# Early-fusion block on one core: inputs handed over in the engines' layout, embedding as six full tiles

## What is computed

```python
patches = im.reshape(B, C, gh, ph, gw, pw).transpose(0, 2, 4, 1, 3, 5).reshape(B, gh * gw, C * ph * pw)
embeds = jnp.einsum('bsp,pd->bsd', patches, W) + b + pos          # 768 values a patch, 192 out
h = jnp.concatenate([cls_tok, embeds, txt], axis=1)
Q = xn[:, None] * W_qk[None, :, None, :]
attn = softmax(causal(Q @ Q.T / sqrt(E)))
out = (attn @ (xn - mean(wte, axis=0))) * N_reg                   # wte: 50257 x 192
h = h + out @ W_o.T
h = h + ffn(layernorm(h))
```

## Time and profile before

| | us |
|---|---|
| median of 3 runs | 526.26 |
| lowest, highest | 524.65, 526.41 |
| profiled execution | 524.14 |
| its span | 522.3 |

### The profile page before, as it was taken

How to read it: one execution, slowest core, us unless ns; L and a number is a source line. 1 busy time by engine, 2 the same in 40 slices (tenths; PEclk the granted TensorE clock), 3 DMA queues, 4 the chain that set the end, 5 groups by cost and what they waited for, 6 DMA issues and landing times.

```text
span 522.3 us, 8913 instructions
## 1 busy us (share of the span) xinstructions
PE 480.4 (92%) x2776; PEld 409.0 (78%) x2776; DVE 332.0 (64%) x868; ACT 178.8 (34%) x575; POOL 66.3 (13%) x93
## 2 busy tenths in 40 slices
PE   0689999999999999999799998779999999999995
PEld 0556666896669866697566997779999999999994
DVE  5584477716675376634863856976666666666764
ACT  0044745604556244733233013312322232223221
POOL 4011111031102011100000143000000000000000
PEclk9977899999999999999987996989999999999997
DMA  9999999489993999995000000011111111111103
GB/s 167 280 177 174 216 214 215 88 158 213 213 211 56 207 213 211 213 203 107 0 1 0 2 20 1 0 31 28 35 38 38 28 35 40 35 28 35 29 1 85
DMA packets 38618, 52.84 MB, mean 101 GB/s; under 512 B 14929, under 2 KB 31318, under 8 KB 38340
## 3 DMA queue, kind: packets, MB, share of 16 engines
q0 software_dynamic: 7664, 39.98, 37.2%
q1 hardware_dynamic: 27612, 10.64, 9.8%
q10 hardware_dynamic: 3320, 1.95, 2.0%
HBM read 50.08 MB, written 1.09 MB: 98 GB/s over the span
## 4 chain that ended last, share of the span: by engine, by line
PE 82%; DVE 10%; ACT 2%; issue 2%; ACTq 1%; DMA 1%; POOL 1%; DVEq 0%
PE bank L930 13%; PE bank L825 11%; PE bank L783 6%; PE bank L729 5%; PE bank L899 4%; PE bank L901 4%; PE bank L902 4%; PE bank L900 4%; PE bank L903 4%; PE bank L731 4%; PE bank L788 3%; PE bank L741 2%; PE bank L742 2%; PE bank L757 2%; PE bank L702 2%; PE bank L691 2%
## 5 line engine op out<-in xcount | busy, mean ns | idle before, releaser
L930 PE MATMUL bank<-wdn,hidT 128*128 128x192 f32 (+1 forms) x408 | 78.9, 330 | 5.9 <-DVE hidT L1179 5.9
L615 ACT ACTIVATE area_b<-bank,bcol 128x356 f32<-128x356 f32 x68 | 38.0, 558 | 132.3 <-PE bank L903 132.3
L1359 DVE SCALAR_TENSOR_TENSOR R<-bank,wts,R 128x192 f32<-128x192 f32 (+1 forms) x204 | 72.6, 411 | 8.2 <-issue 3.6
L930 PEld LDWEIGHTS bank<-wdn,hidT 128*128 128x128 f32 (+1 forms) x408 | 67.6, 184 | 6.5 <-DVE hidT L1179 6.5
L529 ACT ACTIVATE pm<-bank,nmax 128x128 f32<-128x128 f32 x96 | 33.9, 365 | 113.0 <-DVE nmax L1088 113.0
L825 PE MATMUL bank<-woT,oT 128*128 128x192 f32 (+1 forms) x432 | 71.6, 327 | 0.0
L1179 DVE SCALAR_TENSOR_TENSOR hidT<-bank,bcol,area_b 128x356 f32<-128x356 f32 x68 | 40.0, 588 | 48.8 <-PE bank L903 48.8
L825 PEld LDWEIGHTS bank<-woT,oT 128*128 128x128 f32 (+1 forms) x432 | 69.9, 182 | 0.5
L899 PE MATMUL bank<-xah,wah 128*128 128x356 f32 x136 | 54.3, 399 | 0.4 <-DVE lg L1137 0.4
L443 POOL DMA_DIRECT2D wacc<-in_L_attn_wte_dram x26 | 31.5, 1263 | 117.5 <-DMA wacc<-in_L_attn_wte_dram 117.5
L901 PE MATMUL bank<-xah,wal 128*128 128x356 f32 x136 | 45.2, 332 | 0.0
(11 more groups left out here) (197 smaller groups left out, 801.7 us busy)
## 6 DMA issues: line engine op xcount, KB each, us to landing
wacc<-in_L_attn_wte_dram POOLq DMA_DIRECT2D x28, 1344.0 KB, 12.9
wdn<-in_L_ffn_Wd_dram SPq DMA_DIRECT2D x16, 96.0 KB, 1.9
wacc<-wacc POOLq DMA_DIRECT2D x1, 1344.0 KB, 9.6
wra<-in_L_ffn_Wu_dram SPq DMA_DIRECT2D x16, 64.0 KB, 1.8
wrb<-in_L_ffn_Wu_dram SPq DMA_DIRECT2D x32, 32.0 KB, 2.0
wra<-in_L_ffn_Wg_dram SPq DMA_DIRECT2D x16, 64.0 KB, 2.0
wrb<-in_L_ffn_Wg_dram SPq DMA_DIRECT2D x32, 32.0 KB, 2.0
R<-in_L_attn_W_o_dram SPq DMA_DIRECT2D x2, 384.0 KB, 14.0
```

What stands on the lines that cost most here:

```text
L930: last = pe.matmul(o, hidT[:, sl, at:at + rows], wdn[:, k, :], start=True, stop=True)
L1359: last = dve.scalar_tensor_tensor(out=old, in0=src, scalar=wts[0:rows_, 3 * i + t, bass.ds(e, 1)], in1=old, op0=ALU.mult, op1=ALU.add)
```

## The change

The host hands over six inputs in another order of axes. The patches come as `x[pair]`: 128 partitions by six blocks of 128 columns (the 768 values of a patch cut into six, 49 patches of one image and 49 of the other at column 64); the patch weights, the positions (as a table with one row for each output row), the head scales, the text and `W_o` come as they lie in SBUF. So `shift_in`, the turns at L678 to L682, `output_weights` and ScalarE's copies are gone, and each is loaded by one DMA or a few. `embed` is six matmuls of 128 rows, 128 columns of patches and 192 outputs for each pair of images. TensorE starts with 16 matmuls of the mask into a PSUM bank that the first scores overwrite. The query area's memset is on GpSimd instead of VectorE; VectorE clears R's four tail tiles, which `W_o` used to fill. The table's first load waits for `woT` and stands behind the first `rstd`; ten, nine and seven additions replace eight, eight and ten. The reduction into `wbar` is five additions, one behind each of the first five groups of the last pair.

TensorE, start of the program, before: `wqk` and `posx` are the head scales and positions, `z` the normalised rows.

The core of the diff:

```diff
@@ -289,42 +277,26 @@
...
-        def image_in(queue, b):
-
-            for c in range(C):
-                at = (0, PS, 4 * PS)[c]
-                queue.dma_start(ximg[at:at + PS, b].rearrange("p (g w) -> p g w", g=G),
-                                x[b, c].rearrange("(g p) w -> p g w", p=PS)).then_inc(s_x[b // 2], 16)
-            queue.dma_start(ximg[5 * PS:6 * PS, b].rearrange("p (g w) -> p g w", g=G)[:, :, 0:WI - HALF],
-                            x[b, C - 1].rearrange("(g p) w -> p g w", p=PS)[:, :, HALF:WI]).then_inc(s_x[b // 2], 16)
-
...
             def text_in(n, b0, b1):
-                sp.dma_start(hin[NIMG:P, b0:b1, 0, :], txt[b0:b1, 0:TM, :].rearrange("b t e -> t b e")).then_inc(s_text[n], 16)
-                sp.dma_start(hin[0:TAIL, b0:b1, 1, :], txt[b0:b1, TM:NTXT, :].rearrange("b t e -> t b e")).then_inc(s_text[n], 16)
-
-            image_in(sp, 0)
+                sp.dma_start(hin[NIMG:P, b0:b1, 0, :], txt[0:TM, b0:b1, :]).then_inc(s_text[n], 16)
+                sp.dma_start(hin[0:TAIL, b0:b1, 1, :], txt[TM:NTXT, b0:b1, :]).then_inc(s_text[n], 16)
+
+            sp.dma_start(ximg[:, 0], x[0]).then_inc(s_x[0], 16)
             sp.wait_ge(s_zero, 1)
             text_in(0, 0, 2)
             sp.dma_start(hin[NIMG - 1:NIMG, :, 0, :], tok_cls[0].rearrange("a (c e) -> a c e", c=1)
                          .broadcast_to([1, B, E])).then_inc(s_text[0], 16)
-            for b in range(2, B, 2):
-                image_in(sp, b)
+            sp.dma_start(ximg[:, 1], x[1]).then_inc(s_x[1], 16)
             text_in(1, 2, B)
-            tails = txt[:, TM:NTXT, :].rearrange("(i k) t e -> k t i e", k=2)
+            for i in range(2, PAIRS):
+                sp.dma_start(ximg[:, i], x[i]).then_inc(s_x[i], 16)
             for k in range(2):
-                sp.dma_start(htail[TAIL * k:TAIL * k + TAIL, :, :], tails[k]).then_inc(s_text[1], 16)
-
-            for part, rows in ((0, P), (1, 64)):
-                src = W_o[P * part:P * part + rows, :].rearrange("o (q j e) -> o q j e", q=NH // 2, j=2)
-                dst = wo_raw[part][0:rows].rearrange("o (q c) e -> o q c e", c=3)
-                for j in range(2):
-                    sp.dma_start(dst[:, :, j, :], src[:, :, j, 0:P]).then_inc(s_wo, 16)
-                    sp.dma_start(dst[:, :, 2, 64 * j:64 * j + 64], src[:, :, j, P:E]).then_inc(s_wo, 16)
+                sp.dma_start(htail[TAIL * k:TAIL * k + TAIL, :, :], txt[TM:NTXT, k::2, :]).then_inc(s_text[1], 16)
+            sp.dma_start(woT[:], W_o).then_inc(s_wo, 16)
...
@@ -434,6 +406,14 @@
             own.mark(pool.tensor_tensor(nregf[:], nregf[:], shift[:], ALU.add))
             pool.wait_ge(pool_own, own.at)
             pool.memset(wts[:], 1.0).then_inc(s_const, 1)
+            pool.wait_ge(s_const, 1)
+            pool.memset(qb[64:P], 0.0).then_inc(s_pad, 1)
+            pool.wait_ge(s_pad, 3)
+
+            def rstd(n, count):
+
+                pool.wait_ge(var_ready, count)
+                pool.tensor_tensor(rs[:, 0:n], ve[:, 0:n], mhalf[:, 0:n], ALU.pow).then_inc(rstd_ready, 1)
 
             def add_rows(c):
...
@@ -445,26 +425,20 @@
                 else:
                     pool.dma_start(wacc[:, side], wte_v[c]).then_inc(wte_in[side], 16)
 
-            pool.wait_ge(s_x[0], 128)
-            pool.wait_ge(s_tokw, 64)
+            rstd(4, 1)
+            pool.wait_ge(s_wo, 16)
             pool.dma_start(wrest[0:WREST, :], wte[P * WROWS:V, :]).then_inc(wte_rest, 16)
-
-            def rstd(n, count):
-
-                pool.wait_ge(var_ready, count)
-                pool.tensor_tensor(rs[:, 0:n], ve[:, 0:n], mhalf[:, 0:n], ALU.pow).then_inc(rstd_ready, 1)
 
             add_rows(0)
             add_rows(1)
-            rstd(4, 1)
             rstd(4, 2)
-            for c in range(2, 10):
+            for c in range(2, 12):
                 add_rows(c)
             rstd(4, 3)
-            for c in range(10, 18):
+            for c in range(12, 21):
                 add_rows(c)
             rstd(4, 4)
-            for c in range(18, NCHUNK):
+            for c in range(21, NCHUNK):
                 add_rows(c)
             for side in range(2):
...
 
         @block.scalar
         def _(act):
-            for g in range(2):
-                src = tok_W.rearrange("(q g k) e -> g q k e", g=2, k=HALF)[g]
-                act.dma_start(wtok[2 * PS * g:2 * PS * g + 2 * PS], src[0:2 * PS]).then_inc(s_tokw, 16)
-                act.dma_start(wtok[4 * PS + PS * g:5 * PS + PS * g], src[2 * PS:PATCH]).then_inc(s_tokw, 16)
-            image_in(act, 1)
-            act.dma_start(posr[:, 0, :], tok_pos[0, 0:P].rearrange("d h w -> d (h w)")).then_inc(s_pos, 16)
-            act.dma_start(posr[0:64, 1, :], tok_pos[0, P:E].rearrange("d h w -> d (h w)")).then_inc(s_pos, 16)
-            act.dma_start(tokb[:, 0:1], tok_b[0:P].rearrange("(e a) -> e a", a=1)).then_inc(s_pos, 16)
-            act.dma_start(tokb[0:64, 1:2], tok_b[P:E].rearrange("(e a) -> e a", a=1)).then_inc(s_pos, 16)
-            act.dma_start(wqk[:], W_qk).then_inc(s_small, 16)
+            act.dma_start(wtok[:], tok_W).then_inc(s_tokw, 16)
+            act.dma_start(w2[:], W_qk.rearrange("p (c h) -> p c h", c=2)).then_inc(s_small, 16)
+            act.dma_start(postab[:], tok_pos).then_inc(s_pos, 16)
+            act.dma_start(tokb[:], tok_b.rearrange("(a e) -> a e", a=1).broadcast_to([P, E])).then_inc(s_pos, 16)
             act.dma_start(lnw[:], ln_w.rearrange("(a e) -> a e", a=1).broadcast_to([P, E])).then_inc(s_small, 16)
-            for b in range(3, B, 2):
-                image_in(act, b)
 
             def turn_out(b, bt):
...
@@ -559,16 +525,12 @@
...
-            act.wait_ge(s_w2, 2)
+            act.wait_ge(s_w2, 1)
...
             queries_b(0, 0, [2])
-            for c in range(0, NCH, 2):
-                act.wait_ge(s_wops, c // 2 + 1)
-                act.activation(woT[:, c:c + 2, :], bank[4 + (c // 2) % 2][:, 0:2 * E].rearrange("p (c e) -> p c e", c=2),
-                               ACT.Copy).then_inc(s_woT if c + 2 < NCH else proj_read, 1)
             act.wait_ge(xnT_ready, 4)
...
@@ -674,37 +636,18 @@
...
-            pe.wait_ge(s_small, 32)
-            pe.transpose(bank[7][:, 0:NH], wqk[:, 0:P], ident[0:NH, 0:NH])
-            pe.transpose(bank[7][0:64, NH:2 * NH], wqk[:, P:E], ident[0:NH, 0:NH]).then_inc(s_wqps, 1)
-            pe.wait_ge(s_posx, 1)
-            pe.transpose(bank[4][:, 0:P], posx[:, 0, :], ident[:])
-            pe.transpose(bank[4][:, P:E], posx[0:64, 1, :], ident[0:64, 0:64]).then_inc(s_posps, 1)
+            for _ in range(WARM):
+                pe.matmul(bank[0][:, :], identb[:], cmask[:].rearrange("p (a t) -> p a t", a=1).broadcast_to([P, GRP, P]),
+                          start=True, stop=True)
 
             def embed(i):
 
-                pe.wait_ge(s_x[i], 128)
-                pe.wait_ge(s_shift, i + 1)
-                for k in range(HALF):
-                    for half in range(2):
-                        tokens = ximg[:, 2 * i + half, k:k + PS * (G * G - 1) + 1:PS]
-                        last = pe.matmul(emb_bank[i][64 * half:64 * half + G * G, 0:E], tokens, wtok[:, k, :],
-                                         start=(k == 0), stop=(k == HALF - 1))
+                pe.wait_ge(s_x[i], 16)
+                for k in range(KX):
+                    last = pe.matmul(emb_bank[i][:, 0:E], ximg[:, i, k, :], wtok[:, k, :], start=(k == 0), stop=(k == KX - 1))
                 last.then_inc(s_embps, 1)
 
-            def output_weights():
-                pe.wait_ge(s_wo, 16 * 8)
-                pe.wait_ge(s_hin, 2)
-                for c in range(NCH):
-                    if c >= 4 and c % 2 == 0:
-                        pe.wait_ge(s_woT, c // 2 - 1)
-                    for part, rows in ((0, P), (1, 64)):
-                        last = pe.transpose(bank[4 + (c // 2) % 2][:, (c % 2) * E + part * P:(c % 2) * E + part * P + rows],
-                                            wo_raw[part][0:rows, c, :], ident[0:rows, 0:rows])
-                    if c % 2:
-                        last.then_inc(s_wops, 1)
-
-            pe.wait_ge(s_tokw, 64)
+            pe.wait_ge(s_tokw, 16)
             embed(0)
             embed(1)
...
@@ -835,7 +779,6 @@
             scores(0, 0)
             embed(2)
             embed(3)
-            output_weights()
 
...
@@ -886,7 +829,7 @@
...
-            pe.wait_ge(s_woT, NCH // 2 - 1)
+            pe.wait_ge(s_wo, 16)
             pe.wait_ge(s_hin, PAIRS)
...
@@ -996,51 +939,30 @@
...
             dve.memset(hin[:, :, 1, :], 0.0).then_inc(s_zero, 1)
-            own.mark(dve.memset(posx[:], 0.0))
             own.mark(dve.memset(lg[:], 0.0))
             own.mark(dve.memset(scan[:], 0.0))
             own.mark(dve.memset(mv[:], 1.0))
             dve.memset(xb[64:P], 0.0).then_inc(s_pad, 1)
             dve.memset(pT1[:], 0.0).then_inc(s_pad, 1)
-            dve.memset(qb[64:P], 0.0).then_inc(s_pad, 1)
-            dve.wait_ge(dve_own, own.at)
```

(61 more changed lines are left out.)

69 lines of the change are left out of this document (32 added, 37 removed).

## The result

| | before | after |
|---|---|---|
| median, us | 526.34 (4 runs, 524.65 to 527.54) | 502.09 (4 runs, 501.91 to 502.19) |
| profiled execution, us | 524.14 | 502.05 |
| its span, us | 522.3 | 500.2 |

The ratio of after to before is 0.9541, with a 95% interval of 0.9515 to 0.9568: 4.6% faster. The forecast was 503.7 us, its sum 502.6 for the profiled execution.

What follows compares the result with a forecast made beforehand. TensorE, busy 92% of the span, was taken as the bound, so only its waits, slow spells and removable work pay. 8.1+1.4+8.5-1.5+5.0 = 21.5 us off 524.14 gave 502.6, put at 503.7 us, range 498 to 510.

Steps and rivals of the forecast that it cites:

- Start: Program start to VectorE's first embedding addition: at 13.9 instead of 22.0 us, 8.1 us gained, bounds 5.2 and 8.9.
- The memset's move: Query area's memset from VectorE to GpSimd at the start: 4 to 6 us there, done by 12, effect zero.
- Embeddings of images 4 to 7: Behind the first scores: 24 passes take 3.9 instead of 5.38 us, 1.4 us gained on VectorE's chain.
- output weights: Ahead of the second scores: transposes and copies go, and VectorE's 8.51 us wait with them; 8.5 us gained.
- A new slow spell: Behind the second scores TensorE has little work and its clock falls: -1.5 us, bounds 0 and -3.
- Last pair: Five hidden additions replace the output weights' reduction: 5.0 us gained (3.5 waiting, 1.5 clock), at least 2.
- rival 4: Last pair's additions not hidden: 0.76 us of each comes back, 3.8 at most, 507.5 us; chance 0.05.
- GpSimd and the table: Reordered GpSimd queue: third root at 96, its user at 111, covered by 15 us; no effect on time.
- Rival 1: TensorE's clock stays up, neither slow spell occurs: 499.7 us, 498 with the early start bound; chance 0.2.
- the first spell: TensorE's slow clock at the first scores, 5.2 us at half pace; rival 1 took 2.5 us for its absence.
- Rival 2: The 16 matmuls fail to raise the clock, or data land late: 506.6 to 509.6 us; chance 0.2.
- Profiled against median: Sum of 502.6 us raised to 503.7, since before's median stood 2.1 above its profiled execution.

Runs made afterwards that it cites:

- three base kernels: After without the 16 matmuls, constants awaited later, memset first, token counts later: 499.39 us; plus twelve matmuls behind the second embedding, 497.57; or third embedding moved there, 495.85.
- an experiment alone: Kernel before with only the output weights loaded in their final layout by one DMA, without transposes and copies: 517.3 us, ratio 0.9809.
- the second trace: The unchanged kernel after, profiled and timed once more: 501.22 us, ratio 0.9542, span 499.9.
- The experiment: Kernel after with 15 instead of 10 table additions ahead of GpSimd's third reciprocal root: 518.41 us, ratio 0.9876.

## Why the prediction was right, and where it was not

*Start (8.1 predicted, 8.56 measured).* The size was right: the matmuls took 5.45 us where 6.0 were taken, the embedding 1.96 where 2.0 were taken. The view behind it was only half read. The prediction took the 16 matmuls as the given start and looked whether data were in time for them (by 9). It never asked what the start would be without them: the first pair's data are in at 5.5 to 6.1 us (landing by about 9 had been worked out; the second pair's are in at 10.6 to 11.2), and the matmuls delay an embedding that could already run. They cost 5.45 us, and the higher pace gives back 1.67 at the first embedding and 0.3 at the second (12 passes in 2.22 us without the matmuls, in 1.94 with them). In the three base kernels the two embeddings took 2.5, 3.3 and 4.4 us longer than in after, which is more than those 2.0 and still less than 5.45. The term could have been 2.8 us larger in a kernel that doesn't have them; for the kernel as it is, the estimate stands. The memset's move was put at zero and came out at zero, but by the matmuls' cover: on GpSimd it held a VectorE operation up for 3.6 us, which the prediction did not foresee; VectorE was ready at 10.61, 2.83 us before the embedding was.

*Embeddings of images 4 to 7 (1.4; 1.30)* and *output weights (8.5; 8.49)* hold, the second one shown by an experiment alone (7.86). The output weights landed by 26.03 us, inside the 21 to 33.5 worked out from the page's rates (20.4 and 33.2 when the sum is redone), and TensorE's only wait ahead of the loop was 1.33 us for VectorE.

*A new slow spell (-1.5; -1.69).* Right as a price, but not a property of the kernel: it was there in after's first trace and absent in its second one. The sum charged it in full, with 0 as a bound, for the gap behind the second scores; the same gap stood in the second trace without the spell, so the gap alone does not bring it. That the profiled execution paid it is luck, and so is part of how well the sum fits it: in an execution that is spared the spell, this term is off by 1.5 us.

*Last pair (5.0; 5.15)* holds in both directions, and all additions were hidden: rival 4 did not occur.

*GpSimd and the table (0; 0).* The third root was issued at 93.68 where 96 was worked out, its user came at 111.03 where 111 was. (The addition ahead of the root, which the prediction calls the eleventh, is the tenth, seven steps behind the third as its sum has it, and 46+7x6.9 is 94.3; it stood at 92.92.) The experiment shows that the cover is 15.8 us and what happens beyond it.

*Rival 1* did not come about in after, but its price for the first spell was borne out when the gap ahead of it was filled (2.47 of 2.5 us). *Rival 2* had its two causes wrong for this kernel: data and output weights were early, and the 16 matmuls sufficed in every trace. That little was in reserve is right: at 6.42 us they were close to the 6.9 that all 16 take at the low clock, and the embedding behind them still took 1.96 us.

*Profiled against median.* The prediction added 1.1 us to the sum because before's median stood 2.1 above its profiled execution. In after the two are 502.05 and 502.09, so this step added an error of 1.1 us where the sum alone was off by 0.6.
